# Four changes of order and one change of engine in a two-layer gated attention kernel on one core

## The reference

```python
x = x + tanh(g_xattn[0]) * xattn0(layernorm(x), ctx)   # 32 heads, 8 key heads of 128, q and k rms-normed
x = x + tanh(g_ffn[0])   * (clip(xn * sx) @ clip(W * sw)) / (sx * sw)   # scales from max |xn|, max |W|
x = x + tanh(g_xattn[1]) * xattn1(layernorm(x), ctx)   # 16 heads, 4 key heads of 96
x = x + tanh(g_ffn[1])   * experts(layernorm(x))       # 8 experts of rank 16, softmax router

def xattn(latents, context):
    kv = concatenate([context, latents], axis=1)       # 487 rows for each sequence
    q, k, v = latents @ Wq, kv @ Wk, kv @ Wv
    return softmax(q @ k.T * scale) @ v @ Wo
```

## Time and profile before

| | |
|---|---|
| median of three runs | 2694.78 us |
| lowest, highest | 2694.04, 2695.9 us |
| the profiled execution's own time | 2694.31 us |
| its span in the trace | 2692.5 us |
| TensorE busy | 2624.9 us, 97% |
| VectorE busy | 1526.4 us, 57% |
| ScalarE busy | 1285.9 us, 48% |
| GpSimd busy | 1033.2 us, 38% |
| mean granted TensorE clock | 0.995 |

### The profile page before, as it was taken

One profiled execution on the slowest core, in us unless ns is written; L12 is line 12 of the kernel. 1 busy time (PEld: TensorE's weight loads), 2 busy tenths in 40 slices (PEclk: granted clock), 3 DMA queues, 4 the chain that ended last, 5 costly groups with the idle time before them and its releaser, 6 DMA issues. The chain is left out here.

```text
span 2692.5 us, 38860 instructions
## 1 busy us (share of the span) xinstructions
PE 2624.9 (97%) x13508; PEld 2240.5 (83%) x13508; DVE 1526.4 (57%) x2708; ACT 1285.9 (48%) x2846; POOL 1033.2 (38%) x884
## 2 busy tenths in 40 slices
PE   7999999999989999999999999999999999999998
PEld 6788778888888888877888888888898999788887
DVE  7767776454665333346566656656345311777766
ACT  6655664423434333356555555555252312755544
POOL 2555424475353111127555555555300000544430
PEclk9999999999999999999999999999999999999999
DMA  4566565555554233336333333333230222433311
GB/s 168 186 210 200 165 226 194 179 194 186 194 187 140 89 102 94 109 97 191 106 107 106 109 101 106 107 104 96 92 119 0 74 98 79 120 95 81 87 45 55
DMA packets 339049, 336.40 MB, mean 125 GB/s; under 512 B 127232, under 2 KB 275448, under 8 KB 338856
## 3 DMA queue, kind: packets, MB, share of 16 engines
q1 hardware_dynamic: 337768, 331.82, 39.7%
q10 hardware_dynamic: 1088, 2.10, 0.2%
HBM read 237.35 MB, written 96.49 MB: 124 GB/s over the span
## 5 line engine op out<-in xcount | busy, mean ns | idle before, releaser
L45 PE MATMUL pb<-p_ws,p_xs 128*128 128x512 f32 (+1 forms) x1124 | 437.6, 389 | 27.5 <-DVE p_xs L470 10.6
L47 PE MATMUL pb<-p_ws,p_xs 128*128 128x512 f32 (+1 forms) x1124 | 427.9, 381 | 0.0
L46 PE MATMUL pb<-p_ws,p_xs 128*128 128x512 f32 (+1 forms) x1124 | 427.2, 380 | 0.0
L847 POOL TENSOR_TENSOR p_xr<-p_xf 128x512 f32<-128x512 f32 x175 | 249.2, 1440 | 273.6 <-ACT p_xf L1053 161.4
L1759 ACT ACTIVATE at_p<-pb,at_nmax 112x487 f32<-112x487 f32 x256 | 171.1, 669 | 321.8 <-DVE at_nmax L1837 321.7
L1266 DVE TENSOR_TENSOR p_c<-pb,p_c 128x512 f32<-128x512 f32 (+1 forms) x280 | 175.5, 658 | 180.6 <-PE pb L47 179.5
L45 PEld LDWEIGHTS pb<-p_ws,p_xs 128*128 128x128 f32 x1124 | 213.1, 190 | 65.4 <-issue 23.2
L1595 POOL TENSOR_TENSOR at_k<-at_kr,at_k 128x488 fp32r<-128x488 f32 (+1 forms) x94 | 116.5, 1240 | 372.8 <-DVE at_k L1851 372.8
L47 PEld LDWEIGHTS pb<-p_ws,p_xs 128*128 128x128 f32 x1124 | 212.7, 189 | 36.2
L46 PEld LDWEIGHTS pb<-p_ws,p_xs 128*128 128x128 f32 x1124 | 213.4, 190 | 32.1
L1856 DVE TENSOR_TENSOR at_ptlo<-pb,at_pthi 125x448 fp32r<-125x448 f32 (+1 forms) x256 | 148.0, 620 | 93.7 <-ACT at_pthi L1781 93.7
(11 more groups left out here) (268 smaller groups left out, 6434.8 us busy)
## 6 DMA issues: line engine op xcount, KB each, us to landing
p_xf<-xT_d SPq DMA_DIRECT2D x23, 1024.0 KB, 6.0
p_raw<-in_L_xattn_Wq_dram SPq DMA_DIRECT2D x32, 512.0 KB, 4.2
at_raw<-in_L_xattn_Wo_dram SPq DMA_DIRECT2D x64, 256.0 KB, 2.8
xT_d<-p_xf SPq DMA_DIRECT2D x15, 1024.0 KB, 5.2
qT_d<-p_qstage SPq DMA_DIRECT2D x56, 256.0 KB, 2.7
at_qr<-qT_d SPq DMA_DIRECT2D x64, 224.0 KB, 3.1
at_rb<-rT_d SPq DMA_DIRECT2D x64, 224.0 KB, 3.5
at_kr<-kT_d SPq DMA_DIRECT2D x64, 187.5 KB, 2.9
```

The source lines that it names most:

```text
L45: pe.matmul(out, stat_hi, mov_hi, start=start, stop=False)
L46: pe.matmul(out, stat_hi, mov_lo, start=False, stop=False)
L47: return pe.matmul(out, stat_lo, mov_hi, start=False, stop=stop)
L847: pool.tensor_tensor(xr[:, n % 10, 1, :, :], src[:, a[0], HK * a[1]:HK * a[1] + HK, :], src[:, b[0], HK * b[1]:HK * b[1] + HK, :], op).the ...
```

## The change

Five things.

1. `lows_on_pool` holds for w = 0 alone: in passes 1 and 2 VectorE makes the lows of the plain blocks.
2. At the ends of passes 0 and 1 SyncE looks at the next pass's weights before it looks at the stores of values of the same event. The load of x for pair 2 of pass 1 moves from the end of pass 0 to pair 1's first high in pass 1; that of pass 2 stays at the end of pass 1.
3. The second four maxima over the feed-forward weight move from pair 4 of pass 2 to pair 5, the reduction WX after them; the loads that go with them move along.
4. In layer 0's attention `spread_sums(u)` stands ahead of the loads for units u + 2 and u + 3 for u up to 8.
5. In layer 1's attention the highs of unit 1's queries are made ahead of the exponentials of unit 0.

```diff
             def lows_on_pool(w, p, j):
-                return j in (3, 4) and not direct(w, p)
+                return w == 0 and j in (3, 4) and not direct(w, p)
...
                 for k in range(KS):
-                    put(2, 3 + k // 4, 1 + k % 4, "WM", k)
-                put(2, 4, 6, "WX")
+                    put(2, 3 + k // 4 * 2, 1 + k % 4, "WM", k)
+                put(2, 5, 6, "WX")
...
                     for e in order:
+                        if e[0] == "E" and e[1:] in ((0, 13, 3), (1, 13, 3)):
...
+                        if e[0] == "E" and e[1:3] in ENDS[0:2] and e[3] >= 3:
+                            w, j = e[1] + 1, e[3]
+                            if j == 6 and w == 2:
+                                load_xf(w, 2)
+                            sp.wait_ge(y_done, y_at[e[1:]] + 1)
...
                         if e[0] == "X":
...
-                        if e[0] == "E" and e[1:3] in ENDS[0:2] and e[3] >= 3:
-                            w, j = e[1] + 1, e[3]
-                            if j == 6:
-                                load_xf(w, 2)
-                            sp.wait_ge(y_done, y_at[e[1:]] + 1)
...
                             if p + 1 < PAIRS[w]:
-                                if p != 1:
+                                if (w, p) != (2, 1):
                                     load_xf(w, p + 1)
...
-                        if e[0] == "E" and e[1:] == (2, 3, 6):
+                        if e[0] == "E" and e[1:] == (2, 4, 3):
                             for k in range(4, KS):
                                 load_wf(k)
-                        if e[0] == "E" and e[1:] == (2, 5, 1):
+                        if e[0] == "E" and e[1:] == (2, 6, 3):
                             for m in range(4):
                                 load_w(m)
...
                 for u in range(U):
+                    if not flip and u <= NB:
+                        spread_sums(u)
                     if u + 3 < U:
                         load_qk(u + 3)
                     if u + 2 < U:
                         load_v(u + 2)
-                    spread_sums(u)
+                    if not (not flip and u <= NB):
+                        spread_sums(u)
...
                 cut_q(0)
                 yield
+                if flip:
+                    cut_q(1)
                 for h in range(G):
                     exp(0, h)
                     yield
-                cut_q(1)
+                if not flip:
+                    cut_q(1)
```

More of the change, by code:

```diff
@@ L683, in _ @@
                     for e in order:
+                        if e[0] == "E" and e[1:] in ((0, 13, 3), (1, 13, 3)):
+                            w = e[1] + 1
+                            for r in range(4):
+                                sp.wait_ge(bg_stored[r], 16 * w * (N_B // 4))
+                            for j in (0, 1):
+                                h, c = W_PLAIN[j]
+                                sp.dma_start(quads[2 + j][:, :, 0:wide(w)], values_block(w, h, c)).then_inc(ws_loaded[j], 16)
+                        if e[0] == "E" and e[1:3] in ENDS[0:2] and e[3] >= 3:
[3 more added lines that the diff above has]
+                            sp.wait_ge(y_done, y_at[e[1:]] + 1)
+                            if j in (3, 4):
+                                sp.dma_start(wr[j][:, 1, :, 0:wide(w)], values_block(w, 4 - j, j - 3)).then_inc(ws_loaded[j - 1], 16)
+                            else:
+                                sp.dma_start(wr[j][:, 1, :, 0:wide(w)], wsum_d[w][j].rearrange("k p n -> p k n")).then_inc(ws_loaded[j], 16)
+                            if j == 4:
+                                sp.dma_start(wr[2][:, 1, :, 0:wide(w)], wsum_d[w][2].rearrange("k p n -> p k n")).then_inc(ws_loaded[4], 16)
+                            if j == 6:
+                                for m in (0, 1):
+                                    wait_low_v(sp, w, m, HK - 1)
+                                    sp.dma_start(quads[2 + m][:, :, 0:wide(w)], wsum_d[w][3 + m].rearrange("k p n -> p k n")).then_inc(ws_loaded[7 + m], 16)
                         if e[0] == "X":
@@ L728, in _ @@
                             sp.dma_start(v_target(i, h), cb[0:rows(i), p % 2, c, :]).then_inc(v_stored[p % 2], 16)
-                        if e[0] == "E" and e[1:] in ((0, 13, 3), (1, 13, 3)):
-                            w = e[1] + 1
-                            for r in range(4):
-                                sp.wait_ge(bg_stored[r], 16 * w * (N_B // 4))
-                            for j in (0, 1):
-                                h, c = W_PLAIN[j]
-                                sp.dma_start(quads[2 + j][:, :, 0:wide(w)], values_block(w, h, c)).then_inc(ws_loaded[j], 16)
-                        if e[0] == "E" and e[1:3] in ENDS[0:2] and e[3] >= 3:
-                            w, j = e[1] + 1, e[3]
-                            if j == 6:
-                                load_xf(w, 2)
-                            sp.wait_ge(y_done, y_at[e[1:]] + 1)
-                            if j in (3, 4):
-                                sp.dma_start(wr[j][:, 1, :, 0:wide(w)], values_block(w, 4 - j, j - 3)).then_inc(ws_loaded[j - 1], 16)
-                            else:
-                                sp.dma_start(wr[j][:, 1, :, 0:wide(w)], wsum_d[w][j].rearrange("k p n -> p k n")).then_inc(ws_loaded[j], 16)
-                            if j == 4:
-                                sp.dma_start(wr[2][:, 1, :, 0:wide(w)], wsum_d[w][2].rearrange("k p n -> p k n")).then_inc(ws_loaded[4], 16)
-                            if j == 6:
-                                for m in (0, 1):
-                                    wait_low_v(sp, w, m, HK - 1)
-                                    sp.dma_start(quads[2 + m][:, :, 0:wide(w)], wsum_d[w][3 + m].rearrange("k p n -> p k n")).then_inc(ws_loaded[7 + m], 16)
                         if e[0] == "XH" and e[1] >= 1 and e[3] == steps(*e[1:3])[0]:
```

## The result

| | before | changed |
|---|---|---|
| median, of 7 runs each | 2695.74 us | 2686.89 us |
| lowest to highest | 2690.63 to 2698.19 | 2685.83 to 2692.1 |
| ratio, 95% interval | 1 | 0.9973 (0.9963 to 0.9982) |
| the profiled execution, its span | 2694.31, 2692.5 | 2688.13, 2686.3 |

By the ratio, which uses all the runs, the change takes 7.3 us off (4.9 to 10.0); the medians alone differ by 8.85. Forecast were 5.45 us, and 2689.3 against the measured 2686.9, which lies inside both the forecast's own range (2686.5 to 2691.5, near its lower end) and the outer one (2685.0 to 2693.5). It is faster by 0.27%, more than the 0.2% that can be told, though the interval's lower end is 0.18%. Run again beside other kernels it gave the same ratio. The sum was near; one term of it was wrong in its mechanism and two were wrong in size. That the errors cancelled is luck.

What follows compares the result with a forecast made beforehand. TensorE, busy 2624.9 of 2692.5 us, was taken as the bound, so only its 67.6 us idle could be won. Terms -1.8 - 1.3 - 0.5 + 0.35 - 2.2 = -5.45 us gave 2689.3 us, range 2685.0 to 2693.5.

Steps and rivals of the forecast that it cites:

- Start of pass 1: TensorE's 3.15 us wait for pair 1's first low shrinks as GpSimd's pair 2 sums come later: -1.8 us.
- Start of pass 2: Earlier weight loads cut TensorE's wait from 2.43 to 0.5 us, less 0.6 for a later store: -1.3 us in sum.
- The 0.6 for the last store: Start of pass 2: pass 1's last store of values lands later behind loads, holding ScalarE, then TensorE: +0.6 us.
- Pairs with maxima: Pass 2 pairs with feed-forward maxima: VectorE making the plain lows takes 0.5 us off 1.74 us of waits.
- Hole after WX: TensorE's 6.05 us wait behind the reduction stays; two new lows ahead of WX add 0.35 us.
- The rival in which the hole closes: GpSimd's 8.50 us gap is a slot wait; 6.05 us and the slow clock go, giving 2680.9 us; chance 0.08.
- Layer 0's sums: Layer 0's attention: storing inverse sums ahead of the loads shortens SyncE's turn and TensorE's waits: -2.2 us.
- Layer 1's highs: Start of layer 1's attention: moving the queries' highs ahead gives 0, since the keys' high on VectorE is late.
- VectorE as bound: Rival: added lows make VectorE late for product 5 in every pair of passes 1 and 2, 2705.8 us; chance 0.08.
- Boundaries give nothing: Rival: full queue at the starts of passes 1 and 2, so no gain there, 2692.4 us; chance 0.22.

Runs made afterwards that it cites:

- e1: Kernel before with only the order of SyncE's loads and stores at the starts of passes 1 and 2 changed; ratio 0.9988 to before.
- e7: Changed kernel with the load of x for pair 1 of pass 2 issued behind the third block's load; ratio 0.9966 to before.
- e13: Kernel before, unedited, run a third time; 2692.35 us.
- e12: Kernel before, unedited, run once more; 2695.39 us.
- e2: Kernel before with only the lows of plain x blocks of passes 1 and 2 made by VectorE; ratio 0.9993 to before.
- e6: Changed kernel with VectorE's high of unit 1's keys ahead of unit 0's maxima in layer 1's attention; 2680.74 us, ratio 0.9947 to before.
- e11: Changed kernel, unedited, run once more; 2686.66 us, ratio 0.9973 to before.
- e3: Changed kernel with the two attention edits (layer 0's sums, layer 1's queries' high) taken back; ratio 0.9975 to before.
- e4: Changed kernel with GpSimd's one reduction over partitions replaced by a copy of the same tile; ratio 0.9946 to before.
- e5: Changed kernel with GpSimd's reduction and VectorE's chain behind it moved from product (2, 5, 6) to (2, 7, 6); 2677.32 us, ratio 0.9931 to before.

## Why the prediction was right, and where not

**Start of pass 1: right.** 1.12, 1.20 and in e1 1.29 us are left, where the forecast had 1.3. What it missed lies behind the wait: see the clock, below.

**Start of pass 2: the failed step.** The prediction said "the second block is now behind one MB of x and one store, some 3.3 us less". Before, that block was behind one MB of x and one store too, as SyncE's queue of before shows:

```profile
695.82 0.43 SPq L742 DMA_DIRECT2D p_wr<-w1T_d  x1
696.35 0.52 SPq L624 DMA_DIRECT2D p_xf<-xT_d  x1
697.14 0.33 SPq L728 DMA_DIRECT2D vl_d<-p_c  x1
697.52 0.60 SPq L742 DMA_DIRECT2D p_wr<-w1T_d  x1
```

Nothing ahead of it was taken away. Against TensorE it went out 0.7 us earlier (691.75 with TensorE 5.05 us ahead, against 697.52), and needed 9.75 us in place of 9.04. It was priced as if bytes ahead of it had gone, and at the 411 GB/s of a later stretch; from 692 to 702 the transfers moved 270 to 376. (The prediction also calls this block two places behind the load of 695.82; it is three.) e7 does what the prediction had credited, and the wait falls to 0.61, near the forecast 0.5. The 0.6 for the last store came as 0 to 0.46 in the profiles with this order, more (1.44, 2.56) where TensorE is earlier. So the edit gained nothing at its wait and cost up to that much behind it. That the stretch ahead of it still got 1.3 us shorter is from two other things, neither of them in the sum: the wait of 0.2 to 0.65 for a low L1357 (705.65 in e13, 706.29 in e12) is in neither profile of the changed kernel, and in e13 the clock fell at 403. The second is chance. So it is luck that this stretch came near its forecast.

**Pairs with maxima: right cause, size too small.** -1.3 in place of -0.5 by the waits; by place the stretch with both pairs got 2.2 us shorter, and what the rest of that is stays open. I took a third of what was there, since two lows more still stand among the additions; with GpSimd's own lows gone the waits go almost whole. e2 shows that the lows do it and not the move of the maxima.

**Hole after WX: size too small.** +1.1 in place of +0.35, and not from the two lows ahead of WX but from the one behind the gap, 1.78 against 0.68 us. This is the slowing of VectorE's lows beside GpSimd's sums that the prediction itself used at the start of pass 1. The rival in which the hole closes had about the right price, 8.4, for the wrong reason: some 9.1 by place (7 by the medians) when the reduction goes, nothing when GpSimd only has less to do. The gap goes with the reduction wherever it stands: 8.4 to 9.5 us in ten profiles with sums behind it, 6.6 to 7.4 in the three where it comes late, none with the copy. The Trainium skill (GPSIMD Engine Reference, Terminology) has libraries brought into GpSimd's memory at run time. The runs agree with a price of that kind for the one reduction, but none shows that a library is what is loaded.

**Layer 0's sums: right,** -2.8 for -2.2 (-2.3 if all six profiles with the old order are taken); what the old order costs is 0.1 to 3.8 us by execution, and it is luck that the one profile's 2.2 lies near the mean (2.1 over six).

**Layer 1's highs: right,** 3.49 stays; e6 shows the keys' high as the cause. **VectorE as bound: wrong,** no plain pair waits. **Boundaries give nothing: wrong** for pass 1, right for pass 2.

**The clock** was priced only at the hole. It can have a price at each of the longer waits: behind the 3.15 to 3.30 us at the start of pass 1 the granted clock from 401 to 412 was 1.00, 1.00, 0.84 (e13) and 0.69 (e2, twelve matmuls at 0.43 us in place of 0.23: 2.4 us); behind 1.1 to 1.3 us it was 1.00 in all ten profiles with that load's new place. So shortening that wait was worth 2.1 us and, in two of four profiles, up to 2.4 more. At the start of pass 2 a wait of 2.31 to 2.43 us is followed by a stretch at half the clock in 5 of 11 profiles (1 of 4 with the old order there, 4 of 7 with the new; 704 to 714 at 0.83 in the changed kernel, e11 and e1), and in none of the three where the wait is 1.07 or less. It costs 0.9 to 1.5 us: from the wait to the turned block at 718 the changed kernel takes 13.35 and e11 12.75, and e3, e4 and e5, without it, 11.83 to 11.92. Why one execution has it and another hasn't stays open.

## What to carry to other kernels

Before crediting a load with an earlier landing, list what stands ahead of it in the queue in both orders; only what was taken away counts, and the rate is that of the stretch, not of a full queue elsewhere. Where an idle gap's named releaser has long been done, replace the instruction ahead of the gap by a trivial one: one run tells whether the gap is the instruction's own, and then the cure is to move it to where nobody stands behind it. A wait on the path costs its length and, by the luck of the execution, a stretch at half the clock behind it: here 3.3 us less of wait were worth 5.65, and 2.1 us taken off one of 3.2 up to 4.5. And one profile's waits are one draw: two or three profiles of the same kernel tell which of them repeat before a difference of a us is given a cause.

## What the runs showed of the hardware

- GpSimd's reduction over partitions of a 128x1 tile takes 0.38 to 0.78 us and is followed by 6.6 to 9.5 us in which GpSimd does nothing (13 profiles); a copy in its place by none (e4).
- A low of 128x512 on VectorE takes 0.68 us alone, and 1.77 to 1.78 beside six GpSimd sums on end (six profiles).
- The same wait of TensorE can be followed by half the clock in one execution and not in the next: behind 3.15 to 3.30 us in 2 of 4 profiles, behind 2.31 to 2.43 us in 5 of 11, behind 3.49 us in 11 of 11.
- In the ten us from 692 on, soon after SyncE's queue had run empty, the transfers of the changed kernel moved 270 to 376 GB/s with the transfer engines nearly as busy (0.83 to 1.05) as in the ten us after, at 373 to 420 GB/s (1.02 to 1.08). In e11 the queue began with 383 GB/s and fell to 233 to 331 until 700. Whether the empty queue or the kind of transfer makes the rate low was not separated. Two windows of the changed kernel:

```profile
698.00:700.00 2.00, 2.00 (x13) 2.00 (x12) 0.00 (x0) 0.00 (x0) 0.00 (x0) 1.00 0.98 270
...
702.00:704.00 2.00, 2.00 (x13) 1.93 (x12) 1.94 (x4) 2.00 (x6) 0.00 (x0) 1.00 1.06 403
```
